# One program for the projections and position terms of the last layer

## The chip, the cores and the metric

The kernel runs on one core of one Trainium2 chip. Times are device microseconds (us) of one execution. The engines are TensorE (PE, its weight loads are PEld), VectorE (DVE), ScalarE (ACT), GpSimd (POOL) and SyncE (SP), which issues all transfers named here; 16 DMA engines carry them.

## What is computed

The reference applies four residual layers to an image batch `x` of shape 2 x 48 x 48 x 192 (4608 tokens of 192 channels): a neighbourhood attention, two selective-scan layers, and last a full attention with relative positions. Only the front of the last layer is touched:

```python
x = x + L3(group_norm(x))
# in L3: b = 2, n = h * w = 48 * 48, 12 heads of 16 channels
qkv = x @ qkv_w + qkv_b                       # q, k, v
attn = einsum('bqd,bkd->bqk', q * hd ** -0.5, k)
Rh, Rw = rel_pos_h[idx_h], rel_pos_w[idx_w]
rel_h = einsum('bhwc,hkc->bhwk', q, Rh)       # position terms from the rows
rel_w = einsum('bhwc,wkc->bhwk', q, Rw)       # and from the columns
attn = softmax(attn + rel_h[..., :, None] + rel_w[..., None, :])
out = (attn @ v) @ proj_w + proj_b
```

## The kernel before

`build` runs the layers one after the other. Each step is a function with a `Scope` of its own, in which every engine gets a hand-written program that is tied to the others by semaphores; at the end of a scope the semaphores are cleared and all engines meet at a barrier, so no instruction of a step starts before the last transfer of the step before it that SP waits for has landed.

Layer 3 is these steps:

- `group_norm` "gn3" (line 103) writes the normalized image XN, 96 partitions x 2 chunks x 4608 tokens. Its last instructions are the four scalings of lines 157 and 178.
- `v_projection` "l3v" (line 344) loads its weights (line 358), then makes 36 pieces of 128 tokens: two float32 products on PE (line 380, which the trace counts as four matmul instructions) and one addition of the bias on DVE (line 388), over 4 PSUM banks.
- `qk_projection` "l3qk" (line 237) loads its weights (line 269), then makes 8 row blocks, (q or k) x (channel half c) x (image b), each of 5 pieces of 512, 512, 512, 512 and 256 tokens. A piece is two products on PE (line 292, four instructions), on DVE the bias (line 322), on ACT the float16 upper part `hi` (line 340), and on DVE the float16 rest `lo` (line 330). `hi` and `lo` have two buffers each, one per row block in turn; SP stores a finished block in three transfers (line 280, one part goes out twice), and block n waits until the stores of block n - 2 have landed. At the end SP waits for all stores (line 282). The queries stay in SBUF as QF.
- `rel_terms` "l3r" (line 1539) loads two tables (line 1583), subtracts them (line 1643) and clears borders on POOL (lines 1606, 1607). Per channel half it makes 4 rows, (group of heads) x (kind), of 6 pieces each, 48 pieces in all. A piece is five float32 products of 96 columns on PE (line 1622, ten instructions), the upper part on ACT (line 1637) and the rest on DVE (line 1648), over 4 banks; PE waits until DVE has taken piece n - 4. For kind 0 the product reads rows of the image and writes 48 neighbouring places; for kind 1 it reads and writes a column, with a step of 48 places. After each row SP stores four transfers (line 1598); row r waits for the stores of row r - 2.
- `layer3_attention` "l3a" (line 1651) loads keys, queries and terms of the first two heads and, last, the constants `places` (line 1821); PE first waits for those constants, then for `loaded[0]` and `loaded[1]`, and runs the maxima pass and the 24 heads.

## Time and profile before

| | us |
|---|---|
| median of 3 runs | 4721.52 (4720.76 to 4724.44) |
| the profiled execution | 4717.87, its span 4716.0 |
| PE, DVE, ACT, POOL busy over the span | 3464.0, 3572.9, 2692.4, 1536.5 |
| from the end of the last scaling of gn3 (2966.85) to the first load of l3a (3214.39) | 247.5 |
| from there to the first product of l3a (3244.99) | 30.6 |

Times in the rows are counted from the start of the span. The share of busy time over the whole span says little here, since the layers are limited by different engines; the stretch that is changed is 5% of the span and is read by itself. In a timeline row stand the start, the length, the engine, the line, the operation, what it writes and reads, how many instructions the row joins, and in brackets how long the engine was idle before it and what ended that. PEclk is the granted clock of TensorE as a share of 2.4 GHz.

### The profile page before, as it was taken

What the parts mean: (1) busy time and instruction counts of PE and PEld (TensorE: products, weight loads), DVE (VectorE), ACT (ScalarE), POOL (GpSimd) and SP (SyncE); (2) the same over time, 40 slices, a digit from 0 to 9 for tenths busy, and PEclk for the clock granted to TensorE, in tenths of its full rate; (3) what the DMA queues carried; (4) which work ended last, traced back from release to release, by engine and by line L of the source; (5) the groups of instructions that cost most, each with busy time, mean ns of one, the idle gap of its engine ahead of it and who ended that gap; (6) DMA issues with size and microseconds to landing.
All of it is one profiled execution on the core that took longest, in us unless ns stands there. A gap on an engine that the chain in (4) does not pass through costs nothing. (4 is left out here: it accounts for less than half of the span.)

```text
span 4716.0 us, 120406 instructions
## 1 busy us (share of the span) xinstructions
PE 3464.0 (73%) x47313; PEld 1758.2 (37%) x47313; DVE 3572.9 (76%) x3605; ACT 2692.4 (57%) x4414; POOL 1536.5 (33%) x1124
## 2 busy tenths in 40 slices
PE   3898764148777756306777775765999999999996
PEld 2476622012222223101222222451566665666563
DVE  2755455869999936677999993555888888888884
ACT  0366617735555532864545542141888888888883
POOL 0122200059999920007999990000000000000000
PEclk8899977558888878656878887865999999999998
DMA  3433212432222220232222212133112222211213
GB/s 85 97 68 65 39 42 62 120 94 68 61 65 68 57 66 17 89 118 76 71 61 63 65 48 64 59 120 91 52 52 60 57 56 54 55 52 52 52 53 88
DMA packets 165533, 316.14 MB, mean 67 GB/s; under 512 B 71035, under 2 KB 110147, under 8 KB 161392
## 3 DMA queue, kind: packets, MB, share of 16 engines
q1 hardware_dynamic: 164976, 308.38, 24.9%
q8 instruction: 391, 6.41, 0.6%
q14 instruction: 166, 1.36, 0.1%
HBM read 199.70 MB, written 108.02 MB: 65 GB/s over the span
## 5 line engine op out<-in xcount | busy, mean ns | idle before, releaser
L2005 DVE TENSOR_REDUCE l3a_mx<-l3a_mx 128x2 f32<-128x768 f32 x1362 | 1223.9, 951 | 201.9 <-PE l3a_mx L1909 195.5
L1981 ACT ACTIVATE l3a_p<-l3a_s 128x384 f32<-128x384 f32 x2592 | 1158.5, 491 | 159.7 <-PE l3a_s L1931 149.6
L1398 POOL TENSOR_TENSOR l_scan_sc<-l_scan_s,l_scan_repc 128x768 f32<-128x768 f32 x576 | 1032.3, 1840 | 5.8 <-DVE l_scan_s L1376 5.7
L1335 ACT ACTIVATE l_scan_da<-l_scan_da,l_scan_a 128x768 f32<-128x768 f32 x576 | 504.0, 875 | 637.0 <-PE l_scan_da L1259 636.8
L1931 PE MATMUL l3a_s<-l3a_q,l3a_k 125*32 125x384 f16 x10368 | 827.7, 327 | 3.3 <-issue 3.3
L1909 PE MATMUL l3a_mx<-l3a_k,l3a_q 124*32 124x384 f16 x10896 | 717.0, 335 | 36.3 <-DVE l3a_mx L2005 29.4
L1259 PE MATMUL l_scan_dup<-l_scan_du,l_scan_pick 96*128 96x512 bf16 (+1 forms) x1152 | 350.7, 393 | 367.4 <-DMA l_scan_dt<-l_dtp 213.3
L1943 PE MATMUL l3a_o<-l3a_p,l3a_vh 128*32 128x288 f32 x6920 | 579.5, 406 | 3.0 <-issue 2.9
L1389 POOL TENSOR_TENSOR l_scan_bup<-l_scan_dus,l_scan_repb 128x768 f32<-128x768 f32 x192 | 353.1, 1839 | 656.6 <-DMA l_scan_repc<-l_bcp 656.6
L1875 POOL TENSOR_TENSOR l3a_norm<-l3a_out,l3a_spread 128x576 f32<-128x576 f32 x25 | 35.9, 1434 | 1366.8 <-DMA l3a_spread<-l_inverses 1366.8
L1286 PE MATMUL l_scan_y<-l_scan_sc,l_scan_sum 128*32 128x256 f32 x3456 | 450.1, 475 | 10.4 <-POOL l_scan_sc L1398 10.3
L1259 PE MATMUL l_scan_da<-l_scan_dt,l_scan_pick 96*128 96x512 bf16 (+1 forms) x1152 | 344.8, 388 | 146.5 <-DVE l_scan_s L1376 142.6
L1376 DVE TENSOR_TENSOR_SCAN l_scan_s<-l_scan_da,l_scan_s,l_scan_bu 128x768 f32<-128x768 f32 x256 | 450.0, 1797 | 0.3
L1356 DVE TENSOR_TENSOR l_scan_bu<-l_scan_dup,l_scan_repb 128x768 f32<-128x768 f32 x384 | 360.3, 938 | 60.6 <-PE l_scan_dup L1259 35.3
L1909 PEld LDWEIGHTS l3a_mx<-l3a_k,l3a_q 124*32 124x32 f16 x10896 | 290.7, 97 | 300.7 <-DVE l3a_mx L2005 175.9
L1931 PEld LDWEIGHTS l3a_s<-l3a_q,l3a_k 125*32 125x32 f16 x10368 | 312.6, 95 | 177.2 <-ACT l3a_p L1981 5.2
L760 ACT ACTIVATE l0a_p<-l0a_s 128x512 f32<-128x512 f32 x432 | 236.7, 597 | 153.8 <-PE l0a_s L683 147.0
L1259 PEld LDWEIGHTS l_scan_dup<-l_scan_du,l_scan_pick 96*128 96x128 bf16 x1152 | 103.5, 109 | 558.8 <-issue 540.1
L1943 PEld LDWEIGHTS l3a_o<-l3a_p,l3a_vh 128*32 128x32 f32 x6920 | 232.2, 110 | 78.9 <-issue 5.3
L1259 PEld LDWEIGHTS l_scan_da<-l_scan_dt,l_scan_pick 96*128 96x128 bf16 x1152 | 69.3, 102 | 482.6 <-DVE l_scan_s L1376 435.3
L727 DVE TENSOR_REDUCE l0a_m<-l0a_mx 128x2 f32<-128x648 f32 x216 | 179.1, 834 | 78.1 <-PE l0a_mx L668 70.4
L1376 DVE TENSOR_TENSOR_SCAN l_scan_s<-l_scan_da,l_scan_s,l_scan_bup 128x768 f32<-128x768 f32 x128 | 231.1, 1805 | 0.0
(197 smaller groups left out, 4242.6 us busy)
## 6 DMA issues: line engine op xcount, KB each, us to landing
l3a_q<-l_qx SPq DMA_DIRECT2D x104, 486.0 KB
l_scan_du<-l_dup SPq DMA_DIRECT2D x144, 144.0 KB, 2.8
l_scan_dt<-l_dtp SPq DMA_DIRECT2D x144, 144.0 KB, 3.4
l_scan_repb<-l_bcp SPq DMA_DIRECT2D x48, 384.0 KB
l_scan_repc<-l_bcp SPq DMA_DIRECT2D x48, 384.0 KB
l3a_q<-l_hx SPq DMA_DIRECT2D x26, 288.0 KB
l_dtp<-l_prep_high_t SPq DMA_DIRECT2D x16, 432.0 KB, 3.1
l_dup<-l_prep_high_u SPq DMA_DIRECT2D x16, 432.0 KB, 3.1
```

The source lines that it names most:

```text
L1259: mm = pe.matmul(out[:, at:at + w], PICK[:, g, :], src[k % 2][:, tl, at:at + w], start=True, stop=True)
L1286: mm = pe.matmul(y_ps[32 * tl:32 * tl + 32, cols], SUM[:, g, :], SC[:, (tr * NT + tl) % NSC, cols], start=g == 0 and k != 1, stop=g == NG ...
L1335: act.activation(da_ps[st % 2][:, 0:TC], da_ps[st % 2][:, 0:TC], ACT.Exp, scale=A[:, column:column + 1]).then_inc(exped, 1)
L1356: dve.tensor_tensor(BU[:, m % 3, :], du_ps[:, 0:TC], REPB[k % 2][:], ALU.mult).then_inc(multiplied, 1)
L1376: dve.tensor_tensor_scan(way(S[:, n, :], d), way(da_ps[st % 2][:, 0:TC], d), way(bu, d), S[:, n, edge:edge + 1] if chained else 0.0, ALU.m ...
L1389: pool.tensor_tensor(BUP[:, tr % 2, :], DUS[:, tr % 2, :], REPB[k % 2][:], ALU.mult)\
L1398: pool.tensor_tensor(SC[:, st % NSC, :], S[:, n, :], REPC[k % 2][:], ALU.mult).then_inc(weighted, 1)
L1909: mm = pe.matmul(out[32 * c:32 * c + 32, a, 0:RG], Q[h % NB][0:rows, variant(g), at:at + 32], K[h % NB][0:rows, g * RG:(g + 1) * RG], star ...
L1931: mm = pe.matmul(s_ps[g % NS_PS][32 * c:32 * c + 32, 0:SW], K[e % NB][:, keys], Q[e % NB][:, variant(kt * 128 // RG), at:at + SW], start=T ...
L1943: mm = pe.matmul(o_ps[32 * g:32 * g + 32, 0:QG], VH[e % NB][:, kt, :], P[:, k % NP, g * QG:(g + 1) * QG], start=kt == 0, stop=kt == KT - 1)
L1981: act.activation(P[:, k % NP, third * SW:(third + 1) * SW], s_ps[g % NS_PS][:, 0:SW], ACT.Exp)\
L2005: dve.tensor_reduce(MX[:, h % NB, qt, 2 * pair:2 * pair + 2], mx_ps[bank][:, :, 0:RG], AX_X, ALU.max)\
```

## The change

- `group_norm` gets a `preload`: during gn3 SP issues the loads of the weights for q, k and v (one transfer), both biases and both position tables.
- The four scopes from `v_projection` to `rel_terms` become one function, `l3_front`, with one list of 124 pieces of three kinds: "v" (36), "qk" (40) and "rel" (48). The order is: the 10 query pieces of channel half 0; its 24 rel pieces, among which 32 pieces are spread (the 20 key pieces and 12 of v); the 10 query pieces of half 1; its 24 rel pieces, with one of the 24 remaining v pieces behind each.
- PE uses 8 banks (before 4). Before piece n it waits until the bank of piece n - 8 has been read by whoever reads it last.
- DVE does the first operation of piece n and then the last of piece n - 2 (`LAG`). ACT goes through the qk and rel pieces in the list's order. SP stores in the list's order too. The pairs of `hi`/`lo` buffers stay, for the qk blocks and for the rel rows apart.
- QF holds one channel half instead of two.
- In `layer3_attention` PE no longer waits for `loaded[0]` and `loaded[1]` together, but for each where its head begins.

The diff, cut; the removed function is shown above:

```diff
@@ group_norm
-            if load is not None:
+            if load is not None or preload is not None:
-                    load(sp, loaded)
+                    if load is not None:
+                        load(sp, loaded)
+                    if preload is not None:
+                        preload(sp)
-def rel_terms(nc, name, QF, t, qx_dram, hx_dram):
+def l3_front(nc, name, XN, t, w_sb, b_sb, bias, table, last, loaded, n_loads, V, homes, qx_dram, hx_dram):
...
+    NGR = RW // RG
+    NB, LAG, COPIES = 8, 2, 3
...
+        QF = s.sb("qf", [CP, TOK])
+        val = s.sb("val", [CP, 4, CH])
+        hi = s.sb("hi", [CP, 2, L], F16)
+        lo = s.sb("lo", [CP, 2, L], F16)
+        rhi = [s.sb(f"rhi{i}", [CP, B, L], F16) for i in range(2)]
+        rlo = [s.sb(f"rlo{i}", [CP, B, L], F16) for i in range(2)]
+        acc = [s.ps(f"acc{i}", [128, CH]) for i in range(NB)]
+        relative, cleared, ready, valued, rounded, split, v_done = (
+            s.sem(n) for n in ("relative", "cleared", "ready", "valued", "rounded", "split", "v_done"))
         stored = [s.sem(f"stored{i}") for i in range(2)]
+        r_stored = [s.sem(f"r_stored{i}") for i in range(2)]
+        def product(q, c):
+            return [("qk", q, c, b, at, w) for b in range(B) for at, w in LCH]
+        def terms(c):
+            return [("rel", c, grp, kind, g) for grp in range(2) for kind in range(2) for g in range(NGR)]
+        def spread(main, fill):
+            out = []
+            for i, x in enumerate(main):
+                out += [x, *fill[i * len(fill) // len(main):(i + 1) * len(fill) // len(main)]]
+            return out
+        values = [("v", n) for n in range(TOK // 128)]
+        FILL = 12
+        jobs = (product(0, 0) + spread(terms(0), product(1, 0) + product(1, 1) + values[:FILL])
+                + product(0, 1) + spread(terms(1), values[FILL:]))
         J = len(jobs)
...
+        def freed(eng, n):
+            kind = jobs[n][0]
+            if kind == "v":
+                eng.wait_ge(v_done, nth_value[n])
+            elif kind == "qk":
+                eng.wait_ge(valued, nth_qk[n])
+            else:
+                eng.wait_ge(split, nth_rounded[n])
...
+        def buffer_free(eng, n):
+            if jobs[n][0] == "qk":
+                slot = slots[jobs[n][1:4]]
+                if slot >= 2:
+                    eng.wait_ge(stored[slot % 2], 16 * COPIES * (slot // 2))
+            elif jobs[n][4] == 0:
+                kind, row = jobs[n][3], r_rows[jobs[n][1:4]] // 2
+                if row >= 1:
+                    eng.wait_ge(r_stored[kind], 16 * 2 * B * row)
...
+                for n, x in enumerate(jobs):
+                    if x[0] == "qk" and x[4] + x[5] == L:
+                        _, q, c, b, at, w = x
+                        slot = slots[q, c, b]
+                        sp.wait_ge(split, nth_rounded[n])
+                        for part, dst in homes(q, c, b):
+                            sp.dma_start(dst, (hi, lo)[part][:, slot % 2, :]).then_inc(stored[slot % 2], 16)
+                    if x[0] == "rel" and x[4] == NGR - 1:
+                        _, c, grp, kind, g = x
+                        sp.wait_ge(split, nth_rounded[n])
...
+                                sp.dma_start(dst.rearrange("e k l -> k e l"), src).then_inc(r_stored[kind], 16)
+                for i in range(2):
+                    sp.wait_ge(stored[i], 16 * COPIES * len(slots) // 2)
+                    sp.wait_ge(r_stored[i], 16 * 2 * B * len(r_rows) // 2)
...
             def _(pe):
+                pe.wait_ge(loaded, n_loads)
                 pe.wait_ge(relative, 1)
+                for n, x in enumerate(jobs):
+                    if n >= NB:
+                        freed(pe, n - NB)
+                    bank = acc[n % NB]
+                    if x[0] == "qk":
+                        _, q, c, b, at, w = x
+                        for k in range(CC):
+                            mm = pe.matmul(bank[0:CP, 0:w], w_sb[:, k, q * C + c * CP:q * C + (c + 1) * CP],
+                                           XN[:, k, b * L + at:b * L + at + w], start=k == 0, stop=k == CC - 1)
+                    elif x[0] == "v":
+                        tile = x[1]
+                        for k in range(CC):
+                            mm = pe.matmul(bank[:, 0:C], XN[:, k, tile * 128:(tile + 1) * 128], w_sb[:, k, 2 * C:3 * C],
+                                           start=k == 0, stop=k == CC - 1)
+                    else:
+                        _, c, grp, kind, g = x
+                        q = QF[:, :].rearrange("p (b h w) -> p b h w", b=B, w=W)
+                        if g == 0 and grp == 0 and kind == 0:
+                            pe.wait_ge(valued, nth_qk[n])
+                        for i in range(RG):
+                            at = g * RG + i
                             rhs = q[:, :, at, :] if kind == 0 else q[:, :, :, at]
                             lhs = table[:, kind, grp, RW - 1 - at:RW - 1 - at + RK, :].rearrange("p k e -> p (k e)")
+                            mm = pe.matmul(bank[0:CP, i * B * H:(i + 1) * B * H], lhs, rhs, start=True, stop=True)
+                    mm.then_inc(ready, 1)
...
+                for n, x in enumerate(jobs):
+                    if x[0] == "v":
+                        continue
+                    buffer_free(act, n)
+                    if x[0] == "qk":
+                        act.wait_ge(valued, nth_qk[n])
+                        act.activation(qk_home(n, hi), value(n), ACT.Copy).then_inc(rounded, 1)
+                    else:
+                        act.wait_ge(ready, n + 1)
+                        act.activation(rel_home(n, rhi), banked(n), ACT.Copy).then_inc(rounded, 1)
...
             def _(dve):
+                dve.wait_ge(loaded, n_loads)
                 dve.tensor_tensor(table[:], table[:], last[:], ALU.subtract).then_inc(relative, 1)
                 dve.wait_ge(cleared, 4 * B)
+                def front(n):
+                    x = jobs[n]
+                    if x[0] == "rel":
+                        return
+                    dve.wait_ge(ready, n + 1)
+                    if x[0] == "v":
+                        dve.tensor_tensor(V[:, x[1], :, :], acc[n % NB][:, 0:C].rearrange("p (h d) -> p h d", d=HD),
+                                          bias[:].rearrange("p (h d) -> p h d", d=HD), ALU.add).then_inc(v_done, 1)
+                        return
+                    _, q, c, b, at, w = x
+                    dve.tensor_scalar(value(n), acc[n % NB][0:CP, 0:w], b_sb[:, q * CC + c:q * CC + c + 1],
+                                      QUARTER if q else 1.0, ALU.add, ALU.mult).then_inc(valued, 1)
+                def back(n):
+                    x = jobs[n]
+                    if x[0] == "v":
+                        return
+                    dve.wait_ge(rounded, nth_rounded[n])
+                    buffer_free(dve, n)
+                    if x[0] == "qk":
+                        dve.wait_ge(valued, nth_qk[n])
+                        dve.tensor_tensor(qk_home(n, lo), value(n), qk_home(n, hi), ALU.subtract).then_inc(split, 1)
+                    else:
+                        dve.tensor_tensor(rel_home(n, rlo), banked(n), rel_home(n, rhi), ALU.subtract).then_inc(split, 1)
+                for n in range(J + LAG):
+                    if n < J:
+                        front(n)
+                    if n >= LAG:
+                        back(n - LAG)
@@ layer3_attention, PE
-                pe.wait_ge(loaded[0], LOADS)
-                pe.wait_ge(loaded[1], LOADS)
                 for number, h, pos, what in before_loop():
+                    if pos == 0:
+                        pe.wait_ge(loaded[h], LOADS)
@@ build, layer 3
-                    group_norm(nc, "gn3", X, XN, group_mean)
-                    v_projection(nc, "l3v", XN, t["l3_wT"], t["l3_b"], V)
-                    qk_projection(nc, "l3qk", XN, t["l3_wT"], t["l3_b"], l3_homes, q_keep=QF, copies=3)
-                rel_terms(nc, "l3r", QF, t, qx_dram, hx_dram)
...
+                def weights(sp):
+                    sp.dma_start(w_sb[:], t["l3_wT"].rearrange("(k p) n -> p k n", p=CP)).then_inc(w_loaded, 16)
...
+                    sp.dma_start(table[:], t["l3_rel"][0]).then_inc(w_loaded, 16)
+                    sp.dma_start(last[:], t["l3_rel"][1]).then_inc(w_loaded, 16)
+
+                group_norm(nc, "gn3", X, XN, group_mean, preload=weights)
+                l3_front(nc, "l3f", XN, t, w_sb, b_sb, bias, table, last, w_loaded, 16 * 5, V, l3_homes, qx_dram, hx_dram)
```

## Rows read from the trace of the kernel before

**Rows 1.** Windows by stage: us, busy PE, PEld, DVE, ACT, POOL, PEclk, DMA share, GB/s.

```profile
2967.00:2999.00 32.00, 26.38 (x144) 26.09 (x144) 12.83 (x36) 0.00 (x0) 0.00 (x0) 0.84 0.03 8
2999.00:3079.00 80.00, 68.80 (x160) 27.45 (x160) 43.68 (x74) 21.15 (x37) 0.00 (x0) 0.91 0.30 106
3079.00:3103.00 24.00, 0.31 (x2) 0.00 (x0) 4.78 (x9) 1.68 (x3) 4.63 (x6) 0.58 0.34 126
3103.00:3214.00 111.00, 82.63 (x480) 77.46 (x480) 69.75 (x48) 67.87 (x48) 1.63 (x3) 0.58 0.40 124
3214.00:3245.00 31.00, 0.01 (x2) 0.04 (x3) 0.00 (x0) 0.00 (x0) 9.86 (x10) 0.50 0.72 196
```

**Rows 2.** Timeline, from the last scaling to the value pieces.

```profile
2962.34 4.51 ACT L178 ACTIVATE l3n_xn<-g_x,gn_shift,gn_rstd 96x2304 f32<-96x2304 f32 x2 [0.43 <-DVE gn_shift L152]
2971.48 26.38 PE L380 MATMUL l3v_acc<-l3v_w,l3n_xn 96*128 96x192 f32 x144 [10.00 <-DMA l3v_bias<-in_l_b]
2978.40 0.36 DVE L388 TENSOR_TENSOR l_v<-l3v_acc,l3v_bias 128x192 f32<-128x192 f32 x1 [0.29 <-PE l3v_acc L380]
```

**Rows 3.** Timeline, the query blocks of l3qk.

```profile
3002.33 27.82 PE L292 MATMUL l3qk_acc<-l3n_xn,l3qk_w 96*96 96x512 f32 x64 [4.47 <-DMA l3qk_b<-in_l_b]
3010.43 0.75 DVE L322 TENSOR_SCALAR l3q_qf<-l3qk_acc,l3qk_b 96x512 f32<-96x512 f32 x1 [0.37 <-PE l3qk_acc L292]
3012.15 0.75 DVE L322 TENSOR_SCALAR l3q_qf<-l3qk_acc,l3qk_b 96x512 f32<-96x512 f32 x1 [0.37 <-PE l3qk_acc L292]
3015.84 1.67 SPq L280 DMA_DIRECT2D l_qx<-l3qk_hi  x2
3030.14 1.15 ACT L340 ACTIVATE l3qk_hi<-l3q_qf 96x512 f16<-96x512 f32 x2 [8.07 <-DMA l_qx<-l3qk_lo]
```

**Rows 4.** Groups of instructions between 2967 and 3214 us, those of DVE.

```profile
L1648 DVE TENSOR_TENSOR l3r_lo<-l3r_acc,l3r_hi 96x480 f16<-96x480 f32 x48 | 69.8, 1552 | 32.6 <-ACT l3r_hi L1637 32.6
L322 DVE TENSOR_SCALAR l3q_qf<-l3qk_acc,l3qk_b 96x512 f32<-96x512 f32 (+1 forms) x20 | 13.8, 691 | 13.0 <-PE l3qk_acc L292 13.0
L330 DVE TENSOR_TENSOR l3qk_lo<-l3qk_val,l3qk_hi 96x512 f16<-96x512 f32 (+1 forms) x20 | 12.5, 627 | 15.8 <-ACT l3qk_hi L340 15.8
```

**Rows 5.** Timeline, start of the position terms.

```profile
3102.05 0.92 DVE L1643 TENSOR_TENSOR l3r_table<-l3r_table,l3r_last 96x732 f32<-96x732 f32 x1 [19.18 <-DMA l3r_last<-in_l_rel]
3103.11 17.18 PE L1622 MATMUL l3r_acc<-l3q_qf,l3r_table 96*96 96x96 f32 x110 [23.80 <-DVE l3r_table L1643]
```

**Rows 6.** Timeline, pieces of kind 0, then of kind 1.

```profile
3109.84 0.57 ACT L1637 ACTIVATE l3r_hi<-l3r_acc 96x480 f16<-96x480 f32 x1 [1.03 <-PE l3r_acc L1622]
3111.76 0.57 ACT L1637 ACTIVATE l3r_hi<-l3r_acc 96x480 f16<-96x480 f32 x1 [0.28 <-PE l3r_acc L1622]
3113.40 14.65 ACT L1637 ACTIVATE l3r_hi<-l3r_acc 96x480 f16<-96x480 f32 x8 [1.07 <-PE l3r_acc L1622]
3122.90 1.92 PE L1622 MATMUL l3r_acc<-l3q_qf,l3r_table 96*96 96x96 f32 x10 [0.33 <-DVE l3r_lo L1648]
```

**Rows 7.** Windows chosen for TensorE's clock, columns as in rows 1.

```profile
3031.00:3045.00 14.00, 12.45 (x31) 5.00 (x32) 11.52 (x20) 4.79 (x9) 0.00 (x0) 1.00 0.36 124
3045.00:3060.00 15.00, 11.65 (x28) 4.70 (x27) 7.05 (x12) 3.97 (x7) 0.00 (x0) 0.89 0.36 135
3117.00:3118.00 1.00, 1.00 (x8) 1.00 (x6) 1.00 (x1) 1.00 (x2) 0.00 (x0) 0.50 0.97 313
3155.00:3166.00 11.00, 11.00 (x69) 11.00 (x69) 3.28 (x7) 4.18 (x5) 0.00 (x0) 0.50 0.80 250
```

**Rows 8.** Timeline, end of the terms and start of the attention.

```profile
3198.31 6.96 DVE L1648 TENSOR_TENSOR l3r_lo<-l3r_acc,l3r_hi 96x480 f16<-96x480 f32 x3
3205.30 0.87 SPq L1598 DMA_DIRECT2D l_qx<-l3r_hi  x1
3214.39 0.35 SPq L1765 DMA_DIRECT2D l3a_k<-l_kx  x1
3244.99 1.19 PE L1948 MATMUL l3a_o<-l3a_p,l3a_vh 128*32 128x288 f32 x8 [46.81 <-DMA l3a_k<-in_l_places]
```

98 lines of the change are left out of this document (37 added, 61 removed).

## The prediction

> **What bounds the kernel now.** I read the windows by stage first, since the change touches only the stretch from the last scaling of gn3 to the first load of l3a, and no engine works across its barriers. PE is busy 26 of 32 us in the value stage, 69 of 80 in the projection, not at all for some 24 us between projection and terms, and 83 of 111 in the terms [rows 1]. No engine binds all of it: the stretch is a chain of four stages, each with a start, a bound of its own and an end. The timeline then shows what each one costs.
>
> The last scaling ends at 2962.34 + 4.51 = 2966.85, and PE starts on the values at 2971.48, when their weights have landed: 4.6 us [rows 2]. The values take 26.4 us. From 2997.9 to 3002.33 PE waits again, now for the weights of q and k: 4.5 us [rows 2, 3]. The projection takes from 3002.33 to some 3079.3, 77 us, for 61.9 us of PE work (below). The rest is waiting for buffers: the stores of block 0 are issued from 3015.84, and ACT begins block 2 only at 3030.14, 14.3 us later, after 8.07 us of idleness, with DVE and then PE stopped behind it [rows 3]. The DMA share of 0.36 with 106 to 126 GB/s beside 0.97 and 313 GB/s in a store of terms [rows 1, 7] says that these stores use about six of the 16 engines. The last of them and the loading of the tables leave PE idle for 23.8 us, to 3103.11 [rows 5]. The terms run to the end of the last DVE piece, 3198.31 + 6.96 = 3205.27 [rows 8]. Sum: 4.6 + 26.4 + 4.5 + 77 + 23.8 + 102.2 = 238.5 us, which is 3205.27 - 2966.85.
>
> **The work itself, per piece.** PE at full clock: a v piece 0.29 + 0.36 = 0.65 us, the pace at which DVE is released [rows 2]. A qk piece of 512 tokens 3012.15 - 3010.43 = 1.72, so a block of four and a half such pieces 7.74 [rows 3]. A piece of kind 0 0.28 + 0.57 = 0.85 at full and 1.03 + 0.57 = 1.60 at half clock. A piece of kind 1 1.07 + 0.57 = 1.64 at full clock [rows 6] and about the same at half: 69 instructions of both kinds fit into 11.0 us there, 0.16 us each, ten to a piece [rows 7]. So PE needs 36 x 0.65 + 8 x 7.74 + 24 x 0.85 + 24 x 1.64 = 23.4 + 61.9 + 20.4 + 39.4 = 145.1 us at full clock, and 46.8 + 123.8 + 38.4 + 39.4 = 248.4 at half clock (v and qk doubled).
>
> DVE: 12.8 for v [rows 1], twice 13.8 and twice 12.5 for qk, 69.8 for the terms [rows 4], 0.9 for the tables [rows 5]: 136.1 us. The terms are uneven: in the last row three pieces of kind 1 take 6.96 us, so they follow each other every 2.27 (2 x 2.27 + 2.42) [rows 8], and PE at kind 1 goes at just that pace, 1.92 of work and 0.33 of waiting for DVE [rows 6]. Kind 0 costs DVE 0.65: (69.8 - 24 x 2.27) / 24. ACT has 67.9 for the terms [rows 1] and, by one 512 piece of 0.58 [rows 3], some 22 for qk: 90, under both.
>
> **The change, part by part.** The new list holds the same work in one program, so its floor is the largest of 145, 136 and 90: PE. I lay it out in order.
>
> *Start.* The loads move into gn3, where SP is idle and no transfer runs for it; they cost nothing if they land within it, as loads that took under 4 us before do. If they did not, the old 4.6 us would stay. The subtraction of the tables now stands before PE's first product: 3102.05 to 3103.11, 1.06 us [rows 5]. The price of the start lies between 1.06 and the old 4.6; I take 2.0, near the first since only a barrier comes on top. PE starts at 2968.9. POOL's clearing, 6.3 us by the 4.63 + 1.63 of the two windows [rows 1], holds ACT and DVE but not PE, which has eight banks, over 10 us of pieces. With the old four banks it would cost about 3.
>
> *PE.* 145.1, and 3.0 for the first microseconds at half clock (the values took 26.4 for 23.4) [rows 2].
>
> *Waits inside.* Twice PE waits until DVE has written the last query piece: about 0.5 each, 1.0. Block 2 begins as piece 11, about 21 us after the start. Block 0's last `lo` is written at about 15 us, since it waits for the first operations of two further pieces, and its stores land 14.3 us later [rows 3], at about 29. So ACT stands for 8 us, and behind it wait the term pieces on ACT and the second operations on DVE. PE goes on through pieces 12 to 19, which are 9.4 us: stall 0 to 2, I take 1.0. Block 3 meets the same with about 5 us: 0.5. Later blocks come more than 14 us after the stores they need. The extra order on SP costs nothing: the block stores need 8 x 10 us (3015.84 to about 3097) and the rows 8 x 6 us at the 0.9 share, 128 us of the busiest DMA engines against 155 of program. If that cover goes, see the rivals.
>
> *DVE as the bound.* A pair of a kind 1 piece and a v piece costs DVE 2.27 + 0.36 = 2.63 and PE 2.29. In the last 24 pairs half are of kind 1. The twelve lose 0.34 each, 4.1, of which the kind 0 rows after the first six give half back: 2.0. With key pieces between (six of kind 1, eight of q or k) it is 22.6 against 22.1, nothing; with eight v pieces 16.5 against 15.0, which the dense query pieces behind give back. The last piece runs through ACT and DVE behind PE: 2 x 2.4 = 4.9. Together 6.9.
>
> Sum at full clock: 2968.9 + 145.1 + 3.0 + 1.0 + 1.5 + 6.9 = 3126.4 for the last DVE piece, before 3205.27: 78.9 us less.
>
> *The clock.* In the projection PE kept the full clock with 12.45 of 14 us busy; with 11.65 of 15 the mean is 0.89 [rows 7]. In pieces of kind 1 it falls without a gap: at 3117 PE is busy for the whole microsecond at 0.50, and 3155 to 3166 stay at 0.50 with PE busy for all of it [rows 7]. Those pieces take 1.64 us at either clock, so the array itself is partly idle in them. In the new list kind 1 stands between qk or v pieces. Bounds: no fall costs 0; a fall in each of the four stretches with kind 1 doubles the 25.0 us of qk and v work in them (12.0 + 5.2 + 3.9 + 3.9) and costs a warm-up of 3.0 in each of the four stretches that follow them or lead on, 12. I take the warm-ups and a fifth of the 25, less 2 hidden by DVE: 15. The projection's dense pieces are the nearest rows for a third of the list, the terms' for the rest, hence a value between.
>
> Last DVE piece at 3141.4, which is 63.9 us earlier. What follows it is as before: the last stores and the barrier, 3205.30 to 3214.39, the loads of l3a, 30.6 us [rows 8]. *The moved wait in l3a* is worth 0: PE's first product was released by the constants, which SP issues last [rows 8]; the keys and queries it no longer waits for at once are ahead of them in the same queue.
>
> The profiled execution would go from 4717.87 to 4654.0; the median of the runs lies 3.65 above it, so 4657.6, say 4658.
>
> One rule of the Trainium skill would give another result. Its page "TensorE: Matmul & The Clock Gate" (section "Why this matters for your kernels") says that TensorE keeps its full clock as long as no longer idle gap stands between the products, and the new list has none. The row at 3117 speaks against it, with PE busy all through and the clock at half. The same page's section on a second failure mode says that short idle times between groups, from cycling through PSUM banks, make the clock swing. By the first the sum would end at its full-clock value.
>
> **The rivals.** (1) *The clock stays full.* The qk and v pieces keep the array active enough; for it speaks 3031 to 3045, against it 3117. Last DVE piece near 3126, 4643; from 4636 to 4648 with the warm-up and waits a little smaller or larger. (2) *Buffers bound it.* Blocks 2 to 5 wait for stores two blocks back, and the rows' stores queue before them; if four such waits reach PE with 7 us each, or the clock falls in most of the list outside the dense parts, 28 us come on top of the forecast: 4686. For it: 14.3 us per store, the same pair of buffers, SP in list order. Against: eight banks. It decides once a wait is longer than the 9.4 us of pieces ahead. (3) *Slower.* The mixed list never reaches full clock: 2968.9 + 248.4 + 1.0 + 1.5 + 4.9 = 3224.7, 19.4 us later than before, 4741. It decides when over 79 of the 103 us between the two clocks are lost, three quarters of the list at half clock. For it the terms' mean of 0.58 [rows 1], against it 0.84 and 0.91 in the dense stages, which are 85 of the 145 us. (4) *It does not do what it says:* the preloads land late or the overlap is undone by an order of waits, and the gain is that of the removed stage ends only, 23.8 + 4.5 + 2.6 = 31 us less 20 of stores that must still drain: 4710.
>
> **How the numbers follow.** Forecast, 4648 to 4669: 52%. Rival 1: 20%. Rival 2, 4669 to 4700: 23%. Rival 3: 2%. Rival 4: 3%, of which 1% lies within 0.2%. The range from 4636 to 4692 takes in rival 1 and most of rival 2. A difference of 0.2%, 9.4 us, is about what a measurement of this kernel can tell from none. Faster by more 0.97, within 0.01, slower 0.02.
>
> **What would show it.** PE should start about 2 us after gn3 and have no idle gap over 2 us until its last product; from gn3's end to the first load of l3a there should be some 184 us instead of 247.5. Right for the clock step: windows at full clock in the first 20 us and in the second query part, dips in kind 1. ACT should stand 5 to 8 us before block 2 while PE goes on. In the last kind 1 rows DVE should be without a gap. The prediction is wrong if PE waits there for banks longer than DVE's 2.63 a pair, if kind 1 pieces cost ACT or DVE more beside other work, or if SP's stores hold a row.

## The result, and the profile after

The changed kernel takes 4653.18 us (median of 4 runs, 4644.40 to 4666.54), beside 4721.14 us for the kernel before in the same comparison (4717.48 to 4724.44, 4 runs). The ratio is 0.9859, with a 95% interval of 0.9831 to 0.9886: 68.0 us less. The prediction said 4658 with a range of 4636 to 4692. The profiled execution, at 4644.40, is the fastest of the four runs, 8.8 us under their median.

In its trace the stretch begins and ends as follows (timeline: start, duration, engine and line, what it writes from what, count, and in brackets the idle time before it with what ended it). These lines answer to [rows 2] and [rows 8].

```profile
2964.46 4.51 ACT L181 ACTIVATE l3n_xn<-g_x,gn_shift,gn_rstd 96x2304 f32<-96x2304 f32 x2 [0.43 <-DVE gn_shift L155]
...
2969.88 0.92 DVE L1728 TENSOR_TENSOR l3n_table<-l3n_table,l3n_last 96x732 f32<-96x732 f32 x1 [2.56 <-PEq L86]
...
2970.95 18.07 PE L1692 MATMUL l3f_acc<-l3n_xn,l3n_w 96*96 96x512 f32 x40 [7.36 <-DVE l3n_table L1728]
...
3129.50 2.40 DVE L1754 TENSOR_TENSOR l3f_rlo<-l3f_acc,l3f_rhi 96x480 f16<-96x480 f32 x1
...
3141.42 0.35 SPq L1877 DMA_DIRECT2D l3a_k<-l_kx  x1
...
3169.85 1.19 PE L2060 MATMUL l3a_o<-l3a_p,l3a_vh 128*32 128x288 f32 x8 [45.42 <-DMA l3a_k<-in_l_places]
```

From the end of gn3 (2964.46 + 4.51 = 2968.97) to the first load of l3a there are 172.45 us where there were 247.54. The two profiled executions differ by 73.5 us (4717.87 - 4644.40), so the stretch carries all of it. What is left over lies around it: gn3 ended 2.1 us later here than before, and from the first load to the end of the span there are 1501.2 us instead of 1501.6 (4642.6 - 3141.42, 4716.0 - 3214.39).

The windows by stage (length, busy time of PE, PEld, DVE, ACT and POOL, granted clock, DMA share, GB/s) show one program where [rows 1] show four stages: the first query product; its terms with key pieces and a third of the values between; the second query product; its terms with the other values; what DVE still has to do; the stores and l3a's loads.

```profile
2971.00:2990.00 19.00, 18.02 (x40) 7.10 (x40) 10.75 (x18) 5.49 (x10) 5.11 (x7) 0.87 0.06 12
2990.00:3057.00 67.00, 66.18 (x347) 47.70 (x348) 54.09 (x72) 40.01 (x43) 0.00 (x0) 1.00 0.47 157
3057.00:3077.00 20.00, 19.12 (x63) 9.85 (x61) 18.55 (x26) 10.29 (x12) 0.00 (x0) 1.00 0.67 211
3077.00:3125.00 48.00, 46.50 (x336) 45.59 (x336) 35.99 (x48) 31.41 (x24) 0.00 (x0) 1.00 0.50 164
3125.00:3132.00 7.00, 0.00 (x0) 0.00 (x0) 6.90 (x5) 3.24 (x2) 0.00 (x0) 0.57 0.00 0
3132.00:3170.00 38.00, 0.15 (x4) 0.18 (x8) 0.00 (x0) 0.00 (x0) 10.00 (x10) 0.50 0.70 204
```

PE is busy 149.8 of the 154 us from 2971 to 3125, so it is now the bound of the list. The granted clock is at its upper level (1.00, 2.4 GHz) once the first microseconds are over, and stays there. In the terms before it was 0.58 [rows 1]. I had expected falls in the rows of kind 1.

The waits for buffers are there, on ACT: two before query and key blocks where they were forecast, two more before later blocks, and two for the stores of rows near the end (timeline of ACT):

```profile
2999.61 0.63 ACT L1720 ACTIVATE l3f_hi<-l3f_val 96x512 f16<-96x512 f32 x1 [7.87 <-DMA l_qx<-l3f_lo]
...
3007.97 0.63 ACT L1720 ACTIVATE l3f_hi<-l3f_val 96x512 f16<-96x512 f32 x1 [2.01 <-DMA l_qx<-l3f_lo]
...
3023.06 1.15 ACT L1720 ACTIVATE l3f_hi<-l3f_val 96x512 f16<-96x512 f32 x2 [4.45 <-DMA l_kx<-l3f_hi]
...
3038.03 0.63 ACT L1720 ACTIVATE l3f_hi<-l3f_val 96x512 f16<-96x512 f32 x1 [4.80 <-DMA l_kx<-l3f_hi]
...
3104.55 1.48 ACT L1723 ACTIVATE l3f_rhi<-l3f_acc 96x480 f16<-96x480 f32 x3 [2.42 <-DMA l_hx<-l3f_rlo]
...
3114.44 13.80 ACT L1723 ACTIVATE l3f_rhi<-l3f_acc 96x480 f16<-96x480 f32 x6 [3.85 <-DMA l_qx<-l3f_rlo]
```

The four before blocks add up to 19.1 us. In the part of the list where they fall PE waits 0.23 and 0.45 us. Its longest waits are the two for the last query piece:

```profile
2990.08 1.06 PE L1708 MATMUL l3f_acc<-l3f_qf,l3n_table 96*96 96x96 f32 x10 [1.06 <-DVE l3f_qf L1741]
...
3044.04 1.57 PE L1697 MATMUL l3f_acc<-l3n_w,l3n_xn 96*128 96x192 f32 x8 [0.45 <-DVE l3f_rlo L1754]
...
3077.18 1.06 PE L1708 MATMUL l3f_acc<-l3f_qf,l3n_table 96*96 96x96 f32 x10 [1.06 <-DVE l3f_qf L1741]
```

### The profile page after: what moved, and what is told of

The parts are those of the page before. It is cut to its first block and busy times, and to the rows that moved or that the text cites. A ratio compares the mean times of both kernels' runs of the same rounds, so it can differ in the third digit from the quotient of the medians.

```text
span 4642.6 us, 120333 instructions
## 1 busy us (share of the span) xinstructions
PE 3430.9 (74%) x47313; PEld 1715.0 (37%) x47313; DVE 3568.5 (77%) x3605; ACT 2693.0 (58%) x4414; POOL 1536.2 (33%) x1124
```

## The experiments

All eleven kernels compute the whole result. "Front" is the time from the end of gn3 to the first load of l3a, "loads" that from this load to the first product of the maxima; the end of gn3 is taken as the start of the tables' subtraction less 0.91 us (2969.88 - 2968.97), for the kernel before and e2 from the last scaling itself. e8 to e11 are built on one another's findings and carry both improvements of e5 and e6.

| kernel | median of runs, us | ratio to before, 95% | front | loads | stretches of 10 us below full clock, first microseconds and end left out |
|---|---|---|---|---|---|
| before | 4719 to 4724 | 1 | 247.5 | 31.5 | most of the terms |
| changed | 4653.18 | 0.9859 (0.9831-0.9886) | 172.5 | 29.4 | none |
| changed, again | 4649.70 | 0.9835 (0.9818-0.9852) | 173.9 | 30.4 | none |
| e1, loads' waits back | 4659.12 | 0.9855 (0.9835-0.9876) | 183.5 | 33.0 | 3040 to 3080 |
| e2, preload only | 4704.47 | 0.9959 (0.9946-0.9972) | 235.4 | 29.3 | the terms (0.59, 3090 to 3190) |
| e3, separate kinds of work | 4677.80 | 0.9894 (0.9872-0.9915) | 203.1 | 29.9 | 3030 to 3040 (0.69), and in and behind the bare terms |
| e4, four banks | 4696.92 | 0.9958 (0.9944-0.9972) | 222.1 | 29.8 | most |
| e5, three block buffers | 4645.09 | 0.9847 (0.9829-0.9864) | 171.1 | 31.1 | none |
| e6, constants first | 4640.08 | 0.9831 (0.9814-0.9847) | 174.8 | 22.1 | none |
| e7, all ideas at once | 4653.40 | 0.9854 (0.9835-0.9874) | 177.7 | 20.6 | 3050 to 3070, 3130 on |
| e8, e5 and e6 | 4630.67 | 0.9815 (0.9799-0.9831) | 170.9 | 22.0 | none |
| e9, e8 and covered query waits | 4634.18 | 0.9813 (0.9796-0.9829) | 169.2 | 20.8 | 3110 on (0.77, then 0.50) |
| e10, e8 and kind 1 first | 4655.58 | 0.9858 (0.9842-0.9874) | 198.6 | 21.6 | 3050 on (0.91 and 0.94 around the second query product) |
| e11, e8 and one drained wait | 4650.37 | 0.9860 (0.9841-0.9879) | 184.3 | 21.8 | 3090 on |

**The changed kernel once more.** No edit.

> The changed kernel once more, for its spread. From its first profile: 172.5 us from the end of gn3 to the first load of l3a, full clock from 2976 to the last product. Theory: the front is the same in every run and the four times of 4644 to 4667 differ elsewhere (in the scans or the attention); then the stretch is again 171 to 174 us at full clock. Rival: the clock falls in the front in some runs, as the prediction had it; then a slower run shows 180 to 190 us there and windows below 0.9. Median 4648 to 4660.

The front repeats within 1.5 us and the clock is again 1.00. But gn3 itself ends at 2974.84, 5.9 us later than in the first trace, on the same code. Over all the traces with unchanged code before it, it ends between 2960.5 (e8) and 2979.5 (e7). So a single profiled execution says within some 10 us how long the kernel is. A front measured from gn3's own end leaves that part out, and these two agree to 1.5 us; but e1 below, whose code is the same up to the attention, has a front 10 us longer, so one front alone is no proof either. I judge by fronts together with what the trace shows inside them, and by medians of runs.

**e1, the moved wait put back.**

```diff
+                pe.wait_ge(loaded[0], LOADS)
+                pe.wait_ge(loaded[1], LOADS)
                 for number, h, pos, what in before_loop():
-                    if pos == 0:
-                        pe.wait_ge(loaded[h], LOADS)
```

> The changed kernel with the two waits for loaded[0] and loaded[1] put back before the first product of the attention. Theory: worth nothing, since the constants are issued last and release the first product; first load to first product stays 28.4 us (3141.42 to 3169.85 in the changed kernel) within 1 us and the time within the spread. Rival: the moved wait is what made that stretch 28.4 us instead of the 30.6 of before; then it is 30 to 31 us again.

In l3a PE's first product was released by the constants as without the edit, so the moved wait is worth nothing. The length itself is no measure of it: the first product came 32.1 us after the first load, where 28.4 within 1 us was expected, and counted to the maxima the loads took 33.0 us here, 29.4 and 30.4 with the wait moved, 31.5 before. Why the loads took longer here is not shown. What this trace showed besides lies far ahead of the edit, in code that is the same as the changed kernel's. First the chain of one wait for a store through the three engines (timeline), then the windows around it:

```profile
3045.05 0.63 ACT L1720 ACTIVATE l3f_hi<-l3f_val 96x512 f16<-96x512 f32 x1 [7.39 <-DMA l_kx<-l3f_hi]
...
3045.71 0.69 DVE L1752 TENSOR_TENSOR l3f_lo<-l3f_val,l3f_hi 96x512 f16<-96x512 f32 x1 [4.07 <-ACT l3f_hi L1720]
...
3047.02 0.92 PE L1697 MATMUL l3f_acc<-l3n_w,l3n_xn 96*128 96x192 f32 x4 [2.56 <-DVE l3f_rlo L1754]
```

```profile
3030.00:3040.00 10.00, 10.00 (x53) 6.33 (x52) 9.10 (x9) 7.10 (x6) 0.00 (x0) 1.00 0.34 116
...
3050.00:3060.00 10.00, 10.00 (x47) 9.91 (x46) 6.63 (x14) 5.74 (x7) 0.00 (x0) 0.50 0.47 163
3060.00:3070.00 10.00, 10.00 (x47) 9.90 (x46) 8.21 (x8) 7.19 (x4) 0.00 (x0) 0.50 0.69 224
3070.00:3080.00 10.00, 10.00 (x31) 6.49 (x30) 8.00 (x8) 4.62 (x4) 0.00 (x0) 0.67 0.22 71
3080.00:3090.00 10.00, 10.00 (x26) 4.08 (x25) 7.45 (x12) 4.12 (x7) 0.00 (x0) 1.00 0.45 144
```

ACT waits 7.39 us where it waited 4.80 in the first trace; 2.56 of it reach PE, and behind it the clock is at half (1.2 GHz) until the next query product, though PE is busy for all of that time. The front is 9.6 to 11.1 us longer than in the two traces above. So the forecast's fall exists, in some executions, and here it begins behind a wait. e4, e5 and e11 go after this.

**e2, only the loading ahead.** The old four stages, with the weights and tables loaded under gn3:

```diff
-                    group_norm(nc, "gn3", X, XN, group_mean)
-                    v_projection(nc, "l3v", XN, t["l3_wT"], t["l3_b"], V)
+                    group_norm(nc, "gn3", X, XN, group_mean, preload=weights)
+                    v_projection(nc, "l3v", XN, t["l3_wT"], t["l3_b"], V, pre=(w_sb, bias, w_loaded, 16 * 5))
```

> The kernel before, with the loads of weights, biases and position tables moved into gn3 and nothing else. Theory: each of the three loads was bare waiting: 2.6 to 3.5 us at the values, 3.4 at the projection, 3.7 before the terms, together 9 to 11 us: about 4711, ratio 0.998. Rival: SP or the DMA engines delay something else in gn3 or the buffers' waits absorb it: 0 to 4 us.

The front is 12.1 us shorter, a little more than the 9 to 11 I had put on it, and a sixth of the gain (12.1 of 75.1). The median is 0.41% or 19.7 us less (4704.47 beside 4724.18), more than the front explains; where the other 7.6 us lie is not shown. The wait ahead of the terms stays, since it is for the stores:

```profile
2964.72 26.49 PE L389 MATMUL l3v_acc<-l3q_w,l3n_xn 96*128 96x192 f32 x144 [6.30 <-PEq L86]
...
3087.52 17.00 PE L1627 MATMUL l3r_acc<-l3q_qf,l3q_table 96*96 96x96 f32 x110 [22.62 <-DVE l3q_table L1648]
```

**e3, one program, but each kind of work by itself.** (With it goes one more wait of DVE, before its first operation on a query or key piece, for the staging buffer. By the order of DVE's own program it is over when DVE comes to it.)

```diff
-        jobs = (product(0, 0) + spread(terms(0), product(1, 0) + product(1, 1) + values[:FILL])
-                + product(0, 1) + spread(terms(1), values[FILL:]))
+        jobs = (product(0, 0) + product(1, 0) + product(1, 1) + values + terms(0)
+                + product(0, 1) + terms(1))
```

> The changed kernel with its pieces not interleaved: queries of half 0, 20 key pieces, 36 v, 24 terms, queries of half 1, 24 terms; still one program, eight banks, preload (DVE gets one more wait that is always over). Theory: the interleaving carries the larger part: blocks 2 to 5 wait for stores (some 58 us for six blocks instead of 46), terms are bound by DVE and ACT in kind 1 (2.27 a piece) and kind 0 rows cannot catch up: front 190 to 205 us, time 4672 to 4688, 20 to 35 above the changed kernel. Rival: one program without barriers is all of it; front 172 to 178, 4648 to 4660. Clock: if the mixture with qk and v pieces is what kept it full, the bare kind 1 rows show 0.50 after a few microseconds, as before; if the gapless list with eight banks is, they show 1.00.

The front is 203.1 us, 30.6 more than interleaved and 32.3 less than with e2's stages. Taken in this order, the preload gives about 12 of the 75.1 us, the single program 32 and the interleaving 31. The 32 is not divided further: the missing barriers, the eight banks and the new order on DVE come together. The two stretches of bare terms run below full clock (windows of this kernel):

```profile
3070.00:3080.00 10.00, 10.00 (x74) 10.00 (x73) 10.00 (x5) 10.00 (x8) 0.00 (x0) 0.59 0.15 50
...
3130.00:3140.00 10.00, 10.00 (x66) 10.00 (x65) 10.00 (x5) 10.00 (x5) 0.00 (x0) 0.52 0.61 197
```

PE is busy for all of both, as at [rows 7]. It had no wait over 0.2 us since 3035.76 when the clock fell for the first time in these rows, at 3068 (0.99 from 3066 to 3068, 0.50 from 3068 to 3070). With value pieces in between, the same rows of kind 1 kept 1.00 in the changed kernel. That speaks for the pieces in between as what holds the clock. The Trainium skill's page "TensorE: Matmul & The Clock Gate" (section "Why this matters for your kernels") makes idle gaps alone decide. The changed kernel's trace agrees with it; these two rows don't.

**e4, four PSUM banks instead of eight.** (With the same additional wait of DVE as e3.)

```diff
-    NB, LAG, COPIES = 8, 2, 3
+    NB, LAG, COPIES = 4, 2, 3
```

> The changed kernel with four PSUM banks in turn where it has eight (and one more wait of DVE before its first operation on a query/key piece, for the staging buffer). Mine: ACT's waits for the block stores (7.87 us before block 2, 4.45 and 4.80 before blocks 4 and 5 in the trace after) are covered by the pieces that PE has ahead, 9.4 us of them with eight banks and about 4.7 with four. So here PE waits at blocks 2 and 4 or 5, some 3 us or more at once, the granted clock is 0.50 in part of the stretch behind such a wait, and the end of gn3 to the first load of l3a is 185 to 200 us instead of 172 to 174: 13 to 27 us slower than the changed kernel, 4663 to 4677. The rival, that the number of banks weighs nothing because DVE and PE take turns at setting the pace: under 176 us and a time within 3 us of the changed kernel's.

The front is 222.1 us, 49.6 more, far above the 13 to 27 that I had expected. The same wait of ACT before block 2 now goes through at nearly half its length, and other waits of 1.2 to 2.1 us follow (timeline):

```profile
2998.17 0.63 ACT L1720 ACTIVATE l3f_hi<-l3f_val 96x512 f16<-96x512 f32 x1 [7.88 <-DMA l_qx<-l3f_lo]
...
3000.14 3.73 PE L1692 MATMUL l3f_acc<-l3n_xn,l3n_w 96*96 96x512 f32 x4 [3.60 <-DVE l3f_rlo L1757]
...
3074.68 1.87 PE L1708 MATMUL l3f_acc<-l3f_qf,l3n_table 96*96 96x96 f32 x10 [2.09 <-DVE l3f_rlo L1757]
```

Behind the first of them a four-instruction piece of the projection takes 3.73 us, at half clock, where the same row shows 1.88 in the changed kernel. PE's waits add up to about 20 us, against some 4 there; that the rest of the 49.6 is mostly clock is argued from the windows, which are below 1.00 in 15 of the 20 stretches from 2980 to 3180. Eight banks are what makes the interleaving pay: with four the change is worth 0.42%. The additional DVE wait has not been measured by itself.

**e5, a third buffer for the blocks.**

```diff
-        hi = s.sb("hi", [CP, 2, L], F16)
-        lo = s.sb("lo", [CP, 2, L], F16)
+        hi = s.sb("hi", [CP, 3, L], F16)
+        lo = s.sb("lo", [CP, 3, L], F16)
```

> The changed kernel with three buffers instead of two for the high and low halves of the query and key blocks, nothing else. Mine: ACT's waits for block stores (7.87, 2.01, 4.45 and 4.80 us) are mostly gone, PE has no wait over 0.5 us beside those for the two query factors (1.06 each), the granted clock is 1.00 in every stretch of 10 us, and the end of gn3 to the first load of l3a is 168 to 172 us. The time is 4641 to 4650, since the executions in which a wait reaches PE and the clock falls are then gone. The rival, that these waits were covered anyway and what differs from execution to execution lies elsewhere: 172 to 174 us, and the time of the changed kernel within 3 us.

Of ACT's waits for stores one is left, for a row at the end (3.72 us at 3106.15), and PE waits nowhere but for the query factors and once for DVE, 0.75. The front is 171.1, only 1.3 to 2.8 us shorter, the median 4645.09 (4639.08 to 4649.73). In a good execution the waits were covered, as the rival had it. The third buffer takes away the wait from which e1's fall came; that no execution falls any more is not shown. Its runs and those of the changed kernel overlap, so that it is faster is likely, by 4.6 to 8.1 us, and not shown by itself.

**e6, the constants first of l3a's loads.**

```diff
+                for i in range(NB):
+                    sp.dma_start(K[i][3 * HD:KROWS, :], t["l3_places"]).then_inc(consts, 16)
                 for h in range(2):
                     load_keys(sp, h, h)
```

(and the same two lines are gone behind the loop.)

> The changed kernel with the constants of l3a's places loaded first of its loads, ahead of keys, rows and queries of heads 0 and 1. In the traces so far the first product of l3a waits for these constants, which land last (28.4 to 32.1 us after the first load). Mine: the first product comes 17 to 20 us after the first load, released by queries or keys of head 0, and the time is about 11 us less, near 4639. The rival, that head 1's loads or the first softmax then wait for what has been pushed back: the first product is early, and the gain is under 3 us.

The first product comes 11.0 us after the first load, and PE then waits 9.87 us more, for queries, not constants:

```profile
3156.81 1.19 PE L2060 MATMUL l3a_o<-l3a_p,l3a_vh 128*32 128x288 f32 x8 [27.94 <-DMA l3a_k<-in_l_places]
...
3167.87 1.47 PE L2021 MATMUL l3a_mx<-l3a_k,l3a_q 124*32 124x384 f16 x16 [9.87 <-DMA l3a_q<-l_qx]
```

The maxima start 22.1 us after the first load instead of 29.4 or 30.4: 7 to 8 us gained, not 11. The median, 4640.08, is near the 4639 forecast all the same; it is 9.6 and 13.1 us under the two medians of the changed kernel, more than the loads explain. The moved wait may matter here: PE waits for the loads of head 0 only, and transfers still run behind the start of the maxima (DMA share 0.52 from 3170 to 3180). It was not put back to see.

**e7, everything at once.** To e5 and e6 it adds that in each group the row of kind 1 comes before that of kind 0, two value pieces behind each query product, and PE's wait for the subtracted tables only before the first row piece.

> Three block buffers and the constants first (as in the two kernels before this one in the call), and besides: in each group of row pieces the strided kind 1 row before the dense kind 0 row, two value pieces behind each query product, so that PE has work while the query factor is computed, and PE's wait for the subtracted tables stands only before the first row piece. Mine: no wait of 1.06 for the query factors, a tail of DVE behind the last product of about 5 instead of 7.3 us, the end of gn3 to the first load of l3a 163 to 167 us, the first product of l3a about 11 us earlier after its first load, and a time of 4628 to 4634. The rival, that DVE sets the pace wherever a row of kind 1 stands with a value piece: the order within a group weighs nothing, and the time is that of the kernel with the constants first, less at most 2 us.

Neither held: the median is 4653.40 (4638.94 to 4658.01), and the front is 177.7, longer than e5's by 6.6. Its trace shows ACT standing 6.23 us for the store of a row, where it stood for nothing in e5. Behind that PE waits 0.89 and 0.82 us (to 3058.31 and 3062.15), and from 3060 to 3070 the granted clock is 0.56:

```profile
3046.43 2.43 ACT L1724 ACTIVATE l3f_rhi<-l3f_acc 96x480 f16<-96x480 f32 x1 [6.23 <-DMA l_qx<-l3f_rlo]
```

**e8, e9, e10: the parts of e7 one by one.** e8 is e5 and e6 together. e9 and e10 add to it:

```diff
-        jobs = (product(0, 0) + spread(terms(0), product(1, 0) + product(1, 1) + values[:FILL])
-                + product(0, 1) + spread(terms(1), values[FILL:]))
+        jobs = (product(0, 0) + values[:2] + spread(terms(0), product(1, 0) + product(1, 1) + values[2:FILL])
+                + product(0, 1) + values[FILL:FILL + 2] + spread(terms(1), values[FILL + 2:]))
```

is e9 (with PE's wait for the tables moved as in e7), and e10 is

```diff
-            return [("rel", c, grp, kind, g) for grp in range(2) for kind in range(2) for g in range(NGR)]
+            return [("rel", c, grp, kind, g) for grp in range(2) for kind in (1, 0) for g in range(NGR)]
```

> The changed kernel with three buffers for the query and key blocks and with the constants loaded first, nothing else. If the two are independent, the end of gn3 to the first load of l3a is 171.1 us as with the buffers alone, the first product of the maxima comes some 22 us after the first load as with the constants alone (29.7 in the changed kernel), and the time is 4636, some 5 us under each of the two alone. If the gain of one is lost in the other (the loads of l3a start earlier, while stores still run), it is 4640.

> Both of those, and two value pieces behind each query product, with PE's wait for the subtracted tables only before the first row piece. Mine: three waits go (2 x 1.06 for the query factors, 1.0 of the 2.0 at the start), none comes, and the end of gn3 to the first load of l3a is 168 us instead of 171. The rival, that DVE sets the pace after each query product and takes these 3 us back: 171.

> Both of those, and in each group the row of kind 1 before the row of kind 0. Mine, from the trace with all three together, where ACT stood 6.23 us for the store of a row, DVE 5.65 us behind it, and the granted clock was 0.56 between 3060 and 3070: this order alone brings that wait and is what cost the gain; the end of gn3 to the first load of l3a is 176 to 180 us instead of 171, the time 5 to 9 us over that of the kernel without it. The rival, that it was the place of the value pieces: 171 us here.

e8 takes 4630.67 us (4629.90 to 4640.87, 5 runs), the best of all beside e9, and 5 us under its forecast: buffers and constants add up. Two of its five runs are at 4639 and above, so the third buffer does not end the spread.

In e9 the covered waits are worth 1.7 us of front, not 3, and its median is not under e8's. That "none comes" failed: ACT stands 5.47 us for the store of a row, PE waits 1.18 us for what hangs on it, and from there to the end of the list, 6 us, the clock is at half:

```profile
3115.72 1.94 PE L1709 MATMUL l3f_acc<-l3f_qf,l3n_table 96*96 96x96 f32 x10 [1.18 <-DVE l3f_rlo L1755]
```

e10 names the culprit: the order of the kinds alone costs 27.7 us of front and 24.9 us of time, three times the most I had put on it. The wait for a row's store that I expected came (ACT 5.52 us, to 3056.60), with two waits of PE of 0.76 and 1.02 us and 17 us at half clock. The longer part is another: 67 us at half clock behind the wait for the second query factor. With e7 the four make a square: kind 0 first 170.9 without and 169.2 with cover, kind 1 first 198.6 and 177.7, each from one trace. With kind 0 first the 1.06 us wait for the query factors costs next to nothing. With kind 1 first it is followed, in the second part, by half clock to the end of the list; in the first part, where key pieces stand between, the same wait (to 2990.18) is followed by 1.00. The windows of e10 behind the second one, which ended at 3086.38:

```profile
3086.00:3088.00 2.00, 1.62 (x10) 1.65 (x11) 1.44 (x3) 0.42 (x1) 0.00 (x0) 1.00 0.35 136
3088.00:3090.00 2.00, 2.00 (x14) 2.00 (x13) 0.68 (x2) 1.69 (x1) 0.00 (x0) 0.71 0.38 145
3090.00:3095.00 5.00, 5.00 (x25) 4.93 (x24) 4.22 (x3) 4.53 (x3) 0.00 (x0) 0.50 0.38 147
```

In e7, where value pieces stand in place of the wait, the second part is at 1.00 until 3137. Then, behind three waits of PE of 0.75 to 0.76 us within 6 us, it falls too. And in its first part the clock came back by itself, with PE busy and 6 us before the second query product, which starts at 3075.05 (windows of e7):

```profile
3066.00:3068.00 2.00, 2.00 (x9) 1.96 (x8) 2.00 (x2) 0.01 (x1) 0.00 (x0) 0.50 0.40 149
3068.00:3070.00 2.00, 2.00 (x18) 2.00 (x17) 1.91 (x6) 0.57 (x1) 0.00 (x0) 0.80 0.45 173
3070.00:3072.00 2.00, 2.00 (x22) 2.00 (x21) 1.38 (x4) 0.57 (x1) 0.00 (x0) 1.00 0.83 267
...
3130.00:3140.00 10.00, 7.74 (x55) 6.86 (x54) 9.57 (x11) 5.71 (x6) 0.00 (x0) 0.85 0.13 37
```

**e11, one wait put in on purpose.** e8, and before two value pieces PE waits until the piece three places back has left its bank:

```diff
                         tile = x[1]
+                        if tile in (0, FILL + 8):
+                            freed(pe, n - 3)
```

> The kernel with both improvements (three block buffers, constants first), in whose trace the granted clock is 1.00 in every 10 us of the list, and one thing added: before value piece 0 and before value piece 20 PE waits until the piece three places back has left its bank, so that it stands for some 2 us, as it did before value piece 0 in the kernel with the loads' wait put back. Nothing waits for a store there. Mine: it is PE's standing still, whatever made it stand, that brings the half clock. Behind a wait of 2 us or more the granted clock is 0.50 for 20 us or longer, until the next query product, and the list ends 10 us or more later for each of the two; time 4640 to 4652. The rival, that it is not the wait but what the stores do at that moment: the clock stays at 1.00, each wait costs no more than its own length, and the time is 4631 to 4635.

The first of the two turned out to be no wait, since DVE was that far already. The second stood for 3.08 us in the rows of kind 1 of the second part (timeline, then windows):

```profile
3100.88 1.62 PE L1700 MATMUL l3f_acc<-l3n_w,l3n_xn 96*128 96x192 f32 x4 [3.08 <-DVE l3f_rlo L1757]
```

```profile
3080.00:3090.00 10.00, 8.94 (x77) 8.32 (x76) 6.95 (x14) 3.94 (x8) 0.00 (x0) 1.00 0.39 133
...
3098.00:3099.00 1.00, 0.00 (x0) 0.00 (x0) 1.00 (x3) 1.00 (x2) 0.00 (x0) 0.75 0.90 281
...
3110.00:3120.00 10.00, 10.00 (x48) 9.85 (x48) 6.28 (x7) 4.13 (x4) 0.00 (x0) 0.50 0.33 99
3120.00:3130.00 10.00, 10.00 (x51) 9.89 (x50) 3.67 (x8) 1.70 (x3) 0.00 (x0) 0.50 0.21 68
3130.00:3140.00 10.00, 10.00 (x49) 9.89 (x49) 6.59 (x6) 7.83 (x4) 0.00 (x0) 0.50 0.59 179
```

The front is 184.3, 13.4 more than e8's for a wait of 3.08, and the median 19.7 us more. The clock falls within the wait, between 3098 and 3099. No engine waited for a store there. Stores did run (DMA share 0.90), but so they did at the same place in e8 (0.90 and 0.69 in the 4 us from 3080), where PE went on and the clock stayed at 1.00; the added wait is what differs. So a standing PE is enough to bring the half clock in this list, as far as one trace shows. Elsewhere in the list it may be otherwise: in e6 PE stood 1.66 us and the clock stayed at 1.00.

```profile
3044.45 0.92 PE L1697 MATMUL l3f_acc<-l3n_w,l3n_xn 96*128 96x192 f32 x4 [1.66 <-DVE l3f_rlo L1754]
```

## Why the prediction was right

The predicted time was 4.8 us above the median, and most steps held. That it came so near is luck in part, since two errors offset each other: the clock was over-priced in the usual execution, and the profiled execution was taken to lie 3.65 us under the median, where it lay 8.8 under.

*What bounds it, and the list's floor.* Right. PE's work was put at 145.1 us and 3.0 for the first microseconds; busy time is 149.8. PE bounds the list, DVE its end. (One small reading was off: the 106 GB/s of [rows 1] stands beside a DMA share of 0.30, and beside 0.36 stand 124 and 135 [rows 7]. Nothing in the sum hangs on it.)

*Start.* 2.0 forecast, 2970.95 - 2968.97 = 1.98. The loads cost nothing there.

*Waits inside.* For the query factors 1.06 twice, where I had 0.5 twice. ACT's 8 us before block 2 measured 7.87, the 5 before block 3 only 2.01. I had nothing for blocks 4 and 5, "more than 14 us after the stores they need", and there ACT waited 4.45 and 4.80: that step failed. From the first issue of the stores needed (3007.18 and 3020.78) to ACT's start on the block it took 15.9 and 17.3 us, not 14.3, and ACT was there after 11.4 and 12.5. SP issued the stores of a row between the two blocks' (3011.60 to 3020.74); that this is the reason is argued. Before block 5 the cover was half of the 9.4 us of pieces on which I had relied. ACT's waits there of 5.27 us (changed, again), 6.49 (e6) and 7.39 (e1) reached PE as 0.44, 1.66 and 2.56, that is, less 4.83 each time, and 4.80 in the first trace did not reach it there. A reason may be that DVE is behind, so that PE is not ahead by the full eight banks. My sum for the row of kind 1 with eight key pieces, "22.6 against 22.1, nothing", was wrong: by the prices of [rows 4] DVE needs 6 x 2.27 + 8 x 1.315 = 24.1, 2 us more than PE. In e5, where no store holds it, DVE is busy for 20.0 of the 20 us between 3010 and 3030. That this made the cover thin is argued, not shown.

*A sign of being wrong that came.* "SP's stores hold a row" was one, and they did: ACT stood 2.42 and 3.85 us for rows. The sum had nothing for it. PE's only waits behind the first of them are 0.75 us, which e5 has without such a wait, and it has none over 0.2 behind the second.

*DVE as the bound.* A pair of a kind 1 piece and a value piece follows the one before after 2.51 us on DVE, not 2.63 (3129.50 less 3126.99 in the timeline of the changed kernel, below). So PE lost less to it. But at the end DVE was three pairs behind, and the tail is 3131.9 less 3124.4 = 7.5 us instead of 4.9.

```profile
3123.60 0.83 PE L1697 MATMUL l3f_acc<-l3n_w,l3n_xn 96*128 96x192 f32 x4
...
3126.99 2.40 DVE L1754 TENSOR_TENSOR l3f_rlo<-l3f_acc,l3f_rhi 96x480 f16<-96x480 f32 x1
...
3131.93 0.86 SPq L1669 DMA_DIRECT2D l_qx<-l3f_rhi  x1
```

*The sum at full clock.* 159.5 us from the end of gn3 to the last DVE piece (3126.4 - 2966.85); measured 162.9 (3131.90 - 2968.97). The 3.4 are 1.1 for the query factors and 2.6 of tail, less small change.

*The clock.* The mis-sized term. I had put 15 us on it, as something that the rows of kind 1 bring by themselves. Measured: 0 in the two traces of the changed kernel, 10 to 11 in e1's. Rival 1 was right on the mechanism in those two: the pieces in between keep the clock. What I had not seen is the trigger. The rows of [rows 7] that I read as "falls without a gap" are the bare terms, and e3 gives them back (0.52 and 0.59 with PE busy all through); in the mixture every fall in these traces came in or behind a wait of PE, and the clock then stayed down until the next query product (e1, e10) or to the end (e9, e10, e11), but not in e7, where it came back after 10 us. The forecast's front of some 184 us was thus met by e1's 183.5 and missed by the usual 172 to 174.

*The moved wait in l3a.* Worth 0, as said. Whether it is worth something with e6 was not tried.

*Profiled execution and median.* I predicted 4654.0 for the profiled execution and added 3.65. It came out at 4644.4, and its median 8.8 above it. The spread lies partly ahead of the change (gn3's end between 2960.5 and 2979.5), partly, it may be, in whether a store's wait reaches PE, and I can't divide the 8.8 us between the two without traces of the slower runs.

*The rivals.* Rival 2's condition, waits of over 9.4 us, did not come, but the condition was put too high: with eight banks 7.39 us were enough for half clock and 10 us of front in e1. With the banks halved, e4, it was 7.88 us and 4696.92. Rival 3, slower than before, needed three quarters of the list at half clock. Even e4, at half clock for much of it, stayed 0.42% faster. Rival 4 is refuted by the windows.

## What to carry to other kernels

Interleaving dense and thin matrix work in one program pays three times: no barriers, cover for each other's waits, and a full clock for the thin part. It is only as good as the slack behind PE: count the banks, the buffers that wait for stores and how far the following engine really lags, and where there is independent work, put it in place of a wait (e7's second part kept the clock until 3137 where e10's lost it at once; in e8 and e9, with kind 0 first, it mattered little). Before believing a sum of many small gains, try them one by one; here one of four took back more than the other two had given.

## What the runs showed of the hardware

The same mixture of products can run at either clock for a long time. From 3077 to 3125 in the changed kernel value pieces and rows of kind 1 and 0 run at 1.00 with PE busy 46.5 of 48 us; from 3110 to 3140 in e11 the same kinds of pieces run at 0.50 with PE busy 30.0 of 30.

Every fall in a mixed list of eight banks came in or shortly behind a wait of PE: 3.08 us (e11), 2.56 (e1), 1.18 (e9), 0.89 (e7 at 3058), 1.06 with thin work right behind it (e10 at 3086), two waits of 0.76 and 1.02 within 3 us (e10 at 3054), and three of 0.75 to 0.76 within 6 us (e7 at 3137). A single one of 1.66 us in e6 did not bring it, nor did the waits of 1.06 and 0.75 in the changed kernel, so the length of the wait alone does not decide. In the bare terms of e3 it fell at 3068 with PE busy for over 30 us before.

The clock came back with the dense query product in e1 and in e10's first fall, but in e7 it came back after 10 us in kind 0 and value pieces, while in e10 and e11 such pieces stayed at half. What brings it back is open.

The Trainium skill's page "TensorE: Matmul & The Clock Gate" (section "Why this matters for your kernels") promises the full clock to an engine that is kept busy; e11's three windows, busy for all of their 30 us at 0.50, are against it, and the measurement decides. Why the busy engine does not count as such here is not shown by these runs.
